# Row sums of causal attention: folding the second key tile into the first on GpSimd

## The chip, the cores and the metric

The kernel runs on one core of one Trainium2 chip. A core has five engines that run beside each other and meet through semaphores: TensorE (PE) for matmuls, VectorE (DVE), ScalarE (ACT), GpSimd (POOL), and SyncE (SP), which here only issues DMAs. The metric is the device time of one execution in microseconds; lower is better.

## What is computed

One transformer layer in fp32 on an input of 4 x 512 x 1024, with a layer norm after each half:

```python
x = layernorm(x + attention(x, wq, wk, wv, wo))   # 32 heads, 8 kv heads, head size 32, rope, causal
x = layernorm(x + ffn(x))                         # ternary gate/up/down weights with scales, 3584 wide
# attention, per batch b and head h:
scores = q @ k.T / sqrt(32) + causal_mask
attn = softmax(scores)          # exp(scores - max) / sum over the keys
out = attn @ v
```

The division by the sum over the keys is what the change is about. Every softmax row needs the sum of its exponentials over up to 512 keys.

## The kernel before

**Work and units.** The attention stage runs over 16 units `u` (4 batches x 4 groups of 8 heads). A unit has two kv heads `G`, each shared by `REP` = 4 query heads. The 32 pairs (u, G) are numbered `q = u * UG + G`, 0 to 31; the text calls each of them a head. Keys are on the partitions, queries on the free axis. The 512 keys of a head are four key tiles `j` = 3, 2, 1, 0 of 128 keys, worked on in this order. Since the mask is causal, tile j holds only the queries from 128 j on: 128, 256, 384 and 512 columns for each of the four query heads.

**One head.** For each tile TensorE computes scores (`score_k`, L984), ScalarE their exponentials into `p32[j]` (`exp`, L1139), GpSimd sets the upper triangle of the diagonal block to zero (`causal`, L1443), and TensorE multiplies with v (`pv`, L998), in fp32, four query heads on four groups of 32 columns of its array. `p32` has one buffer for each j, so the exponentials of the next head wait until all readers of the old ones are done.

**The row sums.** They are taken by TensorE too: a matmul with a matrix of ones sums over the partitions (`sums`, L1013), again fp32 and four groups of 32 columns. To spare some of it, GpSimd first adds tiles into one another (`presum`, L1451): tile 3 into the fitting columns of tile 2 (512 elements a partition), then tile 2 into tile 1 (1024 elements). So `sums` runs over tiles 0 and 1 only: 4 matmuls of 512 columns and 4 of 384, each recorded twice. The very last head has no presums and sums all four tiles.

```python
tiles = 2
if u * UG + G == NU * UG - 1:
    tiles = NT
else:
    on.wait_ge(s_pre, 2 * (u * UG + G + 1))
```

**After the sums.** VectorE transposes the sums (`sum_turn`, L1291), takes reciprocals (L1296), transposes back (L1298) and multiplies with the result of pv (`att_scale`, L1301). Only then may `pv` of tile 3 of the next head write the PSUM bank again. ScalarE and VectorE split the result into two fp16 parts (L1146, L1307), and SP stores them.

**What else runs there.** Beside the heads TensorE runs the projections of later units (`proj`, L948), scores in the other orientation for the row maxima (`score_q`, L960, L963), whose maxima VectorE takes (`row_max`, L1267), and the output projection of finished batches. VectorE and GpSimd rotate q and k (L1252 to L1254, `rope_add` L1437), ScalarE and VectorE write them as fp16 rows (L1126, L1261), and SP transposes these into the stacks. VectorE also splits incoming pages (L1231). Early on, GpSimd takes a maximum over the partitions once (`bound`, L1468).

**The order.** No engine chooses at run time. A planner in the program (`Plan`) is given every piece of work with its engine, a rank, an estimated duration and the pieces that it comes after. It walks through time and at each moment gives a free engine the ready piece of lowest rank. The resulting order is each engine's program; semaphores then enforce the dependencies. The bank `TRANS`, which `sums` writes, is taken and freed in the plan as well. After attention follows the feed-forward stage, about 740 us to the end.

## Time and profile before

| what | value |
|---|---|
| median of 3 runs (lowest, highest) | 1871.53 us (1870.84, 1872.09) |
| the profiled execution: time, span | 1868.12 us, 1866.4 us |
| mean granted TensorE clock | 0.993 of full speed |
| busy: TensorE, VectorE, ScalarE, GpSimd | 97%, 64%, 38%, 29% of the span |
| ones-matmuls for the sums (L1013), first and last start | 82.5 us, 735.5 us |

The profile is of one execution. "Busy" is the time in which an engine has an instruction running; for TensorE the ends of matmuls are modelled and records overlap. A row of a grouped view gives the line, engine and operation, output and input, how often, the busy time, the mean of one, and the idle time before them with what ended it. A timeline row gives the start and the length in microseconds; where several instructions are merged the length covers them all.

### The profile page before, as it was taken

The page shows a single profiled execution, that of the slowest core. Times are in us where ns is not written, and L with a number is a line of the kernel's source. Part 1 is how long each engine was busy: PE and PEld are TensorE (multiplying, and loading weights), DVE is VectorE, ACT ScalarE, POOL GpSimd, SP SyncE. Part 2 cuts the span into 40 slices and gives each one's busy share as a digit, 9 for nine tenths or more (in the row PEclk, how much of TensorE's full clock was granted, in tenths as well). Part 3 has the DMA queues.
Part 4 walks back from the last instruction along what each step waited for, and adds up shares of the span by engine and source line. Part 5 has one row for each costly group of instructions (what it writes and reads, how often), then busy time and mean ns, then how long its engine had stood idle before and what let it go on. Part 6 is the DMA issues. An engine that isn't in the chain of part 4 may idle for free.

```text
span 1866.4 us, 27364 instructions
## 1 busy us (share of the span) xinstructions
PE 1807.0 (97%) x10528; PEld 882.0 (47%) x10528; DVE 1187.7 (64%) x2047; ACT 710.5 (38%) x1112; POOL 543.6 (29%) x845
## 2 busy tenths in 40 slices
PE   7889999999999998999999999999999999999997
PEld 4545655555555543444444444444444444444443
DVE  7877778668768764445544444745656765667645
ACT  5443444444434444436433343342232322222221
POOL 1354546456546564131000000211321211112103
PEclk9999999999999999999999999999999999999999
DMA  8543234334334398557644353649321211232301
GB/s 246 118 103 78 54 85 125 83 80 116 90 52 114 81 212 221 209 208 263 236 171 150 107 195 126 215 148 211 127 66 53 79 66 51 72 104 85 107 12 79
DMA packets 228162, 233.13 MB, mean 125 GB/s; under 512 B 183872, under 2 KB 184128, under 8 KB 228032
## 3 DMA queue, kind: packets, MB, share of 16 engines
q1 hardware_dynamic: 227168, 230.99, 42.2%
q8 instruction: 83, 1.36, 0.3%
q10 hardware_dynamic: 864, 0.39, 0.1%
q14 instruction: 47, 0.39, 0.1%
HBM read 122.55 MB, written 72.88 MB: 105 GB/s over the span
## 4 chain that ended last, share of the span: by engine, by line
PE 85%; DVE 6%; issue 3%; SPq 2%; POOL 2%; ACT 1%; DMA 1%; ACTq 0%; DVEq 0%; POOLq 0%
PE bank L1053 31%; PE bank L948 20%; PE bank L1074 13%; PE bank L1087 6%; PE bank L998 4%; PE bank L960 3%; PE bank L984 3%; PE bank L1013 2%; SPq L1587 2%; DVE down_forms L1391 1%; PE bank L963 1%; DVE gate_blocks L1385 1%; POOL p_tiles L1451 1%; DVE row_max L1267 0%; DVE up_blocks L1375 0%
## 5 line engine op out<-in xcount | busy, mean ns | idle before, releaser
L1053 PE MATMUL bank<-x_forms,weight_forms 128*128 128x512 f16 x3136 | 700.9, 379 | 12.7 <-DVE gate_blocks L1375 4.4
L1053 PEld LDWEIGHTS bank<-x_forms,weight_forms 128*128 128x128 f16 x3136 | 305.3, 98 | 387.0 <-DVE gate_blocks L1375 7.1
L1139 ACT ACTIVATE p_tiles<-bank 128x512 f32<-128x512 f32 (+1 forms) x352 | 193.0, 556 | 276.6 <-PE bank L984 273.5
L1267 DVE TENSOR_REDUCE row_max<-bank 128x1 f32<-128x384 f32 (+3 forms) x352 | 220.0, 636 | 98.2 <-PE bank L963 96.6
L1074 PE MATMUL bank<-down_forms 128*128 128x512 f16 x1152 | 259.6, 381 | 2.4 <-issue 2.4
L948 PE MATMUL bank<-wq_parts,xT_parts 128*128 128x256 f16 x1536 | 219.4, 275 | 8.9 <-DVE wq_parts L1231 8.7
L1410 DVE TENSOR_TENSOR acc<-bank,acc 128x512 f32<-128x512 f32 x188 | 127.6, 687 | 124.2 <-PE bank L1074 64.7
L1443 POOL TENSOR_SCALAR_AFFINE_SELECT p_tiles<-p_tiles 128x128 f32<-128x128 f32 (+2 forms) x352 | 139.0, 403 | 212.2 <-ACT p_tiles L1139 210.9
L1074 PEld LDWEIGHTS bank<-down_forms 128*128 128x128 f16 x1152 | 113.0, 98 | 139.7 <-issue 4.9
L948 PEld LDWEIGHTS bank<-wq_parts,xT_parts 128*128 128x128 f16 x1536 | 144.1, 98 | 56.8 <-issue 14.2
L948 PE MATMUL bank<-wo_parts,att_parts 128*128 128x512 f16 x672 | 170.1, 382 | 0.6 <-DMA att_parts<-att_spill 0.6
L1475 POOL TENSOR_TENSOR acc<-acc,down_forms 128x1024 f32<-128x1024 f32 x16 | 38.8, 2427 | 377.4 <-DVE acc L1410 377.4
L1087 PE MATMUL bank<-down_forms 128*128 128x512 f16 x560 | 133.6, 379 | 1.7 <-DVE down_forms L1391 1.7
L960 PE MATMUL bank<-k_stack,q_stack 96*128 96x512 f16 (+3 forms) x512 | 127.0, 303 | 5.1 <-DVE row_max L1267 5.1
L984 PE MATMUL bank<-q_stack,k_stack 98*128 98x384 f16 (+3 forms) x512 | 126.4, 301 | 4.6 <-ACT p_tiles L1139 3.1
L1451 POOL TENSOR_TENSOR p_tiles<-p_tiles 128x512 f32<-128x512 f32 (+1 forms) x62 | 115.8, 1868 | 49.4 <-PE bank L998 41.3
L1375 DVE TENSOR_TENSOR up_blocks<-bank,up_blocks 128x512 f32<-128x512 f32 x84 | 57.9, 690 | 112.9 <-PE bank L1053 59.6
L1214 ACT ACTIVATE down_forms<-gate_blocks 128x512 f16<-128x512 f32 x102 | 64.0, 628 | 136.4 <-DVE gate_blocks L1385 130.4
L998 PE MATMUL bank<-p_tiles,v 128*32 128x128 f32 (+3 forms) x1024 | 95.4, 453 | 11.6 <-POOL p_tiles L1443 10.4
L1375 DVE TENSOR_TENSOR gate_blocks<-bank,gate_blocks 128x512 f32<-128x512 f32 x84 | 57.8, 688 | 74.8 <-PE bank L1053 65.0
L948 PE MATMUL bank<-wkv_parts,xT_parts 128*128 128x512 f16 x384 | 98.3, 379 | 1.3 <-DVE wkv_parts L1231 1.3
L1458 POOL TENSOR_SCALAR rstd<-rstd 128x1 f32<-128x1 f32 x96 | 34.8, 363 | 220.2 <-DVE rstd L1329 213.8
(114 smaller groups left out, 1999.9 us busy)
## 6 DMA issues: line engine op xcount, KB each, us to landing
weight_forms_spill<-weight_forms SPq DMA_DIRECT2D x28, 896.0 KB, 5.7
weight_forms<-weight_forms_spill SPq DMA_DIRECT2D x28, 896.0 KB, 4.5
x_forms_spill<-x_parts SPq DMA_DIRECT2D x56, 256.0 KB, 2.4
w_page<-gateT SPq DMA_DIRECT2D x28, 512.0 KB, 5.0
w_page<-upT SPq DMA_DIRECT2D x28, 512.0 KB, 4.0
w_page<-downT SPq DMA_DIRECT2D x28, 512.0 KB, 4.3
att_spill<-att_made SPq DMA_DIRECT2D x64, 128.0 KB, 2.1
down_forms<-x_spill SPq DMA_DIRECT2D x16, 512.0 KB, 3.4
```

The lines of the kernel that those rows point to most:

```text
L948: t = nc.tensor.matmul(dst, left[:, a, k, rows], right[:, c, k, cols], start=k == 0 and m == 0, stop=last)
L960: nc.tensor.matmul(to[:, h, :], qT[0:STK, u % QS, h0 + h, i * P:n], kT[0:STK, b % 2, kv_of(u, h0 + h), 0:n], start=h == 0, stop=False, ski ...
L984: t = nc.tensor.matmul(to[:, h, :], kT[0:STKM, b % 2, (u % UNITS) * UG + G, lo:lo + P], qT[0:STKM, u % QS, G * REP + h0 + h, lo:S], start= ...
L998: t = nc.tensor.matmul(bank[PV_BANK[q]][h * HD:(h + 1) * HD, lo:S], value, p32[j][:, h, :], start=j == NT - 1, stop=j == 0, tile_position= ...
L1053: t = nc.tensor.matmul(strassen[bank_set(use)][to][:, :], w_form[:, use % 4, A_FORMS[a_form], k * P:(k + 1) * P], xF[:, :, B_FORMS[b_form] ...
L1074: t = nc.tensor.matmul(to[:, :], hid_p[place_of(r)][:, k, a, i // 2 * P:(i // 2 + 1) * P], wd_p[place_of(r)][:, c, cols], start=r == round ...
L1087: t = nc.tensor.matmul(to[:, :], hid_f[r % NF % 3][:, HID_FORMS.index(a_form), a, pair * P:(pair + 1) * P], wd_f[r % NF % 3][:, DOWN_B[b_f ...
L1139: nc.scalar.activation(p32[j][:, h0:h0 + heads, :], bank[5 + m % 2][:, 0:heads * n].rearrange("p (h c) -> p h c", c=n), ACT.Exp, scale=SCO ...
L1267: nc.vector.tensor_reduce(mx[:, u % 2, i, h0:h0 + ROW_HEADS[i]], bank[3 + m % 2][:, 0:ROW_HEADS[i] * n].rearrange("p (h c) -> p h c", c=n) ...
L1410: nc.vector.tensor_tensor(dst, got[:, :], dst, ALU.add).then_inc(s_acc, 1)
L1443: nc.gpsimd.affine_select(out=block, in_=block, compare_op=ALU.is_ge, fill=0.0, base=0, pattern=[[0, KEY_HEADS[j]], [1, P]], channel_multi ...
L1451: nc.gpsimd.tensor_tensor(to, to, p32[j + 1][:, :, :], ALU.add).then_inc(s_pre, 1)
```

## The change

For the first 29 of the 32 heads GpSimd now also adds tile 1, which already holds tiles 2 and 3, into the last 384 columns of tile 0. It does so in two instructions, for two query heads each (768 elements a partition). `sums` then runs over tile 0 only, and waits for both. Heads 29 and 30 keep two presums and two tiles, head 31 keeps none and four. The exponentials of tile 1 of the next head wait for the second half instead of the sums; those of tile 0 still wait for the sums. In the plan `sums` gets other durations and a later rank, and the new pieces are planned at 0.2 + 768/410 us each.

```diff
+EARLY = NU * UG - 3
+PRE_EARLY, PRE_LATE = [(2, 0), (1, 0), (0, 0), (0, 1)], [(2, 0), (1, 0)]
+PRE = [PRE_EARLY if q < EARLY else PRE_LATE if q < NU * UG - 1 else [] for q in range(NU * UG)]
+PRE_BASE = [sum(len(p) for p in PRE[:q]) for q in range(NU * UG + 1)]
+def summed(q):
+    return min([j for j, _ in PRE[q]], default=NT - 1) + 1
+def added(q, j):
+    return max([p for p in PRE[q] if p[0] == j - 1], default=None)
...
-        freed = [("pv", *last, j), ("sums", *last) if j < 2 else ("presum", *last, j - 1)] if q else []
+        freed = [("pv", *last, j), ("presum", *last, *added(q - 1, j)) if added(q - 1, j) else ("sums", *last)] if q else []
...
-        final = q == NU * UG - 1
-        if j in (1, 2) and not final:
-            put(PO, at + 4, .2 + REP * (S - (j + 1) * P) / 410, "presum", u, G, j,
-                after=[("pv", u, G, j)] + [("presum", u, G, 2)] * (j == 1))
+        for n, part in enumerate(PRE[q]):
+            if part[0] == j:
+                cols = REP * (S - (j + 1) * P) / (1 if j else 2)
+                put(PO, at + 4, .2 + cols / 410, "presum", u, G, *part,
+                    after=[("pv", u, G, j)] + ([("presum", u, G, *PRE[q][n - 1])] if n else []))
...
-        put(PE, at + 3.5, 3.0 if final else 1.5, "sums", u, G, takes="T", after=[("causal", *one)] + [("presum", u, G, 1)] * (not final))
+        put(PE, at + (7 if summed(q) == 1 else 3.5), (.9, 1.6, 2.2, 2.5)[summed(q) - 1], "sums", u, G, takes="T",
+            after=[("causal", *one)] + ([("presum", u, G, *PRE[q][-1])] if PRE[q] else []))
...
-                    tiles = 2
-                    if u * UG + G == NU * UG - 1:
-                        tiles = NT
-                    else:
-                        on.wait_ge(s_pre, 2 * (u * UG + G + 1))
+                    q = u * UG + G
+                    tiles = summed(q)
+                    on.wait_ge(s_pre, PRE_BASE[q + 1])
...
-                    if j < 2:
+                    if q and added(q - 1, j):
+                        on.wait_ge(s_pre, PRE_BASE[q - 1] + PRE[q - 1].index(added(q - 1, j)) + 1)
+                    else:
                         on.wait_ge(s_sums, q)
-                    else:
-                        on.wait_ge(s_pre, 2 * q - (j - 2))
...
-                    u, G, j = which
+                    u, G, j, n = which
                     q = u * UG + G
+                    heads = slice(0, REP) if j else slice(n * REP // 2, (n + 1) * REP // 2)
                     on.wait_ge(s_pv, NT * q + NT - j)
-                    on.wait_ge(s_pre, 2 * q + 2 - j)
-                    to = p32[j][:, :, P:S - j * P]
-                    nc.gpsimd.tensor_tensor(to, to, p32[j + 1][:, :, :], ALU.add).then_inc(s_pre, 1)
+                    on.wait_ge(s_pre, PRE_BASE[q] + PRE[q].index((j, n)))
+                    to = p32[j][:, heads, P:S - j * P]
+                    nc.gpsimd.tensor_tensor(to, to, p32[j + 1][:, heads, :], ALU.add).then_inc(s_pre, 1)
```

## Rows read from the trace of the kernel before

**Rows 1.** Windows, two stretches of attention: busy us (records) by engine, clock, DMA share, GB/s

```profile
200.00:300.00 100.00, 97.66 (x801) 55.01 (x798) 77.19 (x147) 43.13 (x77) 51.26 (x87) 1.00 0.33 80
...
130.00:140.00 10.00, 8.66 (x79) 4.92 (x77) 9.86 (x17) 5.58 (x10) 7.27 (x9) 1.00 0.98 250
```

**Rows 2.** Waits of TensorE's matmuls in 120:700: total us, times, longest

```profile
PE bank L960 <- DVE row_max L1267: 4.3, 5, 1.5
```

**Rows 3.** Groups by line and form, whole span

```profile
L1451 POOL TENSOR_TENSOR p_tiles<-p_tiles 128x1024 f32<-128x1024 f32 x31 | 74.0, 2386 | 12.1 <-PE bank L998 11.2
...
L1437 POOL TENSOR_TENSOR rope_cos<-rope_cos,rope_sin 128x256 f32<-128x256 f32 x80 | 68.9, 861 | 78.1 <-DVE rope_sin L1254 77.9
...
L1261 DVE TENSOR_TENSOR stack_rows<-rope_cos,stack_rows 128x256 f16<-128x256 f32 x80 | 51.8, 648 | 11.7 <-ACT stack_rows L1126 11.5
...
L1451 POOL TENSOR_TENSOR p_tiles<-p_tiles 128x512 f32<-128x512 f32 x31 | 41.9, 1350 | 37.3 <-PE bank L998 30.1 <-issue 7.2
...
L1013 PE MATMUL bank<-p_tiles,ones 128*32 128x512 f32 x256 | 34.3, 609 | 0.0
...
L1307 DVE SCALAR_TENSOR_TENSOR att_made<-over_sum,att_made 128x512 f16<-128x512 f32 x32 | 27.3, 852 | 4.9 <-ACT att_made L1146 4.5
L1013 PE MATMUL bank<-p_tiles,ones 128*32 128x384 f32 x256 | 26.5, 486 | 0.0
```

**Rows 4.** The chain of work around one head's sums: start us, us, what

```profile
402.04 0.33 PE bank L948 x3
402.36 0.99 PE bank L998 x8
403.36 1.50 PE bank L1013 x16
```

**Rows 5.** Timeline of TensorE: pv, sums and neighbours, six stretches

```profile
93.24 1.51 PE L998 MATMUL bank<-p_tiles,v 128*32 128x384 f32 x8 [3.59 <-POOL p_tiles L1443]
...
193.83 1.69 PE L1013 MATMUL bank<-p_tiles,ones 128*32 128x512 f32 x16
...
209.43 1.69 PE L1013 MATMUL bank<-p_tiles,ones 128*32 128x512 f32 x16
...
334.66 1.06 PE L998 MATMUL bank<-p_tiles,v 128*32 128x512 f32 x8
...
336.09 1.71 PE L1013 MATMUL bank<-p_tiles,ones 128*32 128x512 f32 x16
337.73 0.83 PE L948 MATMUL bank<-wq_parts,xT_parts 128*128 128x256 f16 x6
...
402.29 1.07 PE L998 MATMUL bank<-p_tiles,v 128*32 128x512 f32 x8
403.18 1.69 PE L1013 MATMUL bank<-p_tiles,ones 128*32 128x512 f32 x16
404.79 0.50 PE L948 MATMUL bank<-wq_parts,xT_parts 128*128 128x256 f16 x3
...
408.57 0.86 PE L998 MATMUL bank<-p_tiles,v 128*32 128x128 f32 x16
```

**Rows 6.** Timeline of GpSimd: the start, and two moments of later heads

```profile
91.70 0.37 POOL L1468 PARTITION_ALL_REDUCE scale_bounds<-scale_bounds  x1 [7.00 <-issue]
...
100.60 3.74 POOL L1451 TENSOR_TENSOR p_tiles<-p_tiles 128x512 f32<-128x512 f32 x2 [7.17 <-issue]
...
200.26 1.26 POOL L1451 TENSOR_TENSOR p_tiles<-p_tiles 128x512 f32<-128x512 f32 x1 [0.68 <-PE bank L998]
...
406.22 0.41 POOL L1443 TENSOR_SCALAR_AFFINE_SELECT p_tiles<-p_tiles 128x256 f32<-128x256 f32 x1 [2.59 <-ACT p_tiles L1139]
```

**Rows 7.** Timeline of VectorE: a split of attention rows, the end of a scaling

```profile
200.28 1.79 DVE L1307 SCALAR_TENSOR_TENSOR att_made<-over_sum,att_made 128x512 f16<-128x512 f32 x1
...
406.71 0.69 DVE L1301 TENSOR_TENSOR over_sum<-bank,over_sum 128x512 f32<-128x512 f32 x1
```

**Rows 8.** Line L1261: min/median/max ns, first and last start

```profile
L1261 DVE TENSOR_TENSOR stack_rows<-rope_cos,stack_rows x80: 376/425/2569, 17.5 to 661.9; 128x256 f16<-128x256 f32 x80
```

More of the change, by code:

```diff
@@ L879, in attention_over @@
             on.wait_ge(s_exp, NU * NKEY)
-            on.wait_ge(s_pre, 2 * (NU * UG - 1))
+            on.wait_ge(s_pre, PRE_BASE[-1])
             on.wait_ge(s_sums, NU * UG)
```

## The prediction

> **What bounds the kernel now.** The page comes first: TensorE is busy for 97% of the span, GpSimd for 29%. Then the windows, because a share over the whole span hides the stages. The change lies in the attention stage, from about 65 to 740 us. There TensorE is busy for 97.66 of 100 us at 200:300, VectorE for 77.19, GpSimd for 51.26; only in short stretches, as at 130:140, does TensorE fall to 8.66 of 10, with VectorE at 9.86 [rows 1]. So between 140 and 700 us a microsecond of TensorE work taken away is nearly a microsecond of time, unless another engine's chain gets in front. The waits say how near the others are: in 120:700 the largest wait of TensorE's matmuls is 4.3 us, for the row maxima of VectorE [rows 2]. Before 140 us TensorE does stand behind GpSimd and VectorE.
>
> **Removed: the ones-matmuls of the second key tile.** The sums of a head are 16 records for two key tiles of 512 and 384 columns. By form, the 384-column ones are busy 26.5 us in 32 heads [rows 3], 0.83 us a head, but four column groups run at once and the records' ends overlap. The chain of work counts the set of 16 as 1.50 us [rows 4]. By columns that is 1.50 x 384/896 = 0.64 us for the second tile. I take 0.64, since chain pieces follow one another without overlap; 0.83 is the upper bound. 29 heads x 0.64 = 18.6 us (at most 24.1).
>
> **Moved: the sums.** They now wait for both halves on GpSimd, which start when pv of tile 0 is done, so they can't stand right behind pv 0 any more. The timeline has both cases. Adjacent: pv starts at 402.29, the sums at 403.18, the next fp16 matmul at 404.79, together 2.50 us. Apart, with three matmuls of a projection between: 334.66 to 337.73, 3.07 us [rows 5]; such a three is 0.33 us in the chain [rows 4]. 3.07 - 0.33 - 2.50 = 0.24 us for going into the 32-column fp32 matmuls and out once more. 6 of the 32 sums stand apart already, all in the first 29; for 23 it is new: 23 x 0.24 = 5.5 us lost. Against that, later sums make the scaling late, and with it pv of tile 3 of the next head (all heads but the last share one PSUM bank for pv). By then pv of tile 2 is ready too and both run in one go, as the 16 records at 408.57 do [rows 5]. 11 heads do that now, 18 of the first 29 could join; if 12 do, 12 x 0.24 = 2.9 us come back (bounds 0 and 4.3).
>
> **Added: two GpSimd adds a head.** The trace has no add of 768 elements. Between 1350 ns for 512 and 2386 ns for 1024 [rows 3], which are also its bounds, it is 1868 ns. 58 x 1.87 = 108 us on GpSimd, 3.7 us a head. Their cover is GpSimd's idle time: 51 of 100 us busy becomes about 70, and behind pv 0 it now sits idle for 2.59 us until 406.22 [rows 6]. Without the cover the price would be the 108 us themselves. What they make late: the exponentials of tile 1 of the next head on ScalarE, which wait for the second half instead of the sums; the sums, behind them VectorE's chain to the end of the scaling at 407.40 (2.6 us after the sums) [rows 7], then pv 3. Queued behind a waiting add on GpSimd are the causal masks of tiles 3 and 2, rope adds (and with them the hi and lo rows and SP's transposes into the q stack) and the small steps of the layer norm. One head's loop: adds 3.7 us with 1.9 us of masks and a rope add between them, sums 1.0, scaling 2.6, pv 3 and pv 2 0.8, pv 1 0.8, the presum of tile 1 2.4, hand-offs 1.5: 14.7 us until the next adds can start. Heads follow each other in (336.09 - 193.83)/7 = 20.3 us on average, at the shortest in 209.43 - 193.83 = 15.6 us [rows 5]. So the loop fits, with over 5 us of slack in most heads and 1 us in the shortest. I price it at 1 us in all (bounds 0 and 4).
>
> **The start.** Here GpSimd is the limit. It stands for 7.00 us before the all-reduce of the scale bounds and for 7.17 us before its next add [rows 6], and TensorE waits 3.59 us for a mask behind the first of them [rows 5]. The adds of head 0 come in just there. In front of these stalls they move all that is behind by 3.7 us; in a gap they cost nothing. I take 3.7, because GpSimd's queue has no gap between 84.7 and 105.8 but the stalls; with the adds of heads 1 and 2, in the stretch where VectorE is at 9.86 of 10, it could be 8.
>
> **VectorE behind the adds.** VectorE instructions with both inputs in SBUF are stretched under GpSimd's adds. The subtraction for the stack rows has a median of 425 ns, a minimum of 376 and a maximum of 2569 [rows 8]; one of the attention rows that starts at 200.28 lasts 1.79 us [rows 7], where a GpSimd add had started at 200.26 [rows 6]. The two forms, 80 x (0.648 - 0.376) and 32 x (0.852 - 0.679), lose 27 us under 74.0 + 41.9 + 68.9 = 185 us of GpSimd adds [rows 3]. 108 us more of them would be 16 us more of VectorE, 0.5 us a head, on an engine busy for 77 of 100. I let TensorE stand for 2 of these 16 us; the bounds are 0 and 16. The Trainium skill, page "SBUF — State Buffer", section "Who interferes with whom", says that a VectorE instruction with two SBUF inputs and a GpSimd instruction that reads SBUF block one another for the whole instruction. By that rule, the trace agrees, and it would give the third rival's time if every new add met such an instruction, against 2 us in the sum here.
>
> **The sum.** -18.6 + 5.5 - 2.9 + 1 + 3.7 + 2 = -9.3 us. The last three heads are as before, so the end of the stage moves as a whole, and the feed-forward stage keeps its work. The profiled execution took 1868.12 us (span 1866.4) and becomes 1858.8. The median of the runs shown lies 3.4 us above it at 1871.53; with the same distance the prediction is 1862.2 us.
>
> **Rivals.** *First, the hand-offs cost nothing:* the late sums find their place, the start hides head 0's adds. -18.6 + 5.5 - 4.3 = -17.4 us, with the upper price of the matmuls -23: 1849 to 1854 us. For it: TensorE nearly always has other matmuls to run. Against it: the start. *Second, it comes out even:* start 8, loop 4, VectorE 4 us: -16.0 + 16 = 0, 1871.5 us. For it: heads with 1 us of slack, and VectorE near full at 130:140 [rows 1]. Against it: 5 us of slack in most heads. *Third, slower, VectorE held by the adds:* each of the 58 adds meets a subtraction or split of VectorE and holds it for half an add, 58 x 0.93 = 54 us of VectorE. The row maxima queued behind come late, free their two score banks late, and TensorE stands for half of it, 27 us. -16.0 + 3.7 + 27 = +15 us, 1886 us. It decides once TensorE stands for more than 12 of the 54 us. For it: the stretched instructions [rows 7, 8], and that TensorE's largest wait is for the row maxima. Against it: that wait is only 4.3 us under all the adds that there are now [rows 2].
>
> **How the numbers follow.** This kernel's measurement tells about 0.2%, 3.7 us, from no change. The forecast, 4 to 15 us faster, gets 0.52; the first rival 0.14, the second 0.18, the third 0.16. So faster 0.66, same 0.18, slower 0.16. The likeliest case alone spans 1856 to 1867 us. The range for 8 in 10 takes in part of the first rival, the second, and what of the third lies just beyond it: 1851 to 1876 us.
>
> **What would show it.** Right: ones-matmuls of 384 columns in the last three heads only, 2.5 us instead of 26.5; sets of 8 records of about 0.86 us in the chain; 58 adds of 768 elements at 1.8 to 2.0 us; the sums 4 to 7 us behind pv 0; TensorE still at 97 to 100 of 100 us from 140 to 660. Wrong: a wait for the row maxima above 12 us in 120:700 (third rival); the heads after 110 us more than 4 us later than now (the start); pv 3 waiting for the scaling in many heads (the loop). A planner fixes the order on every engine from estimated durations, so the new pieces may also swap larger ones, which no step here prices.

## The result, and the profile after

The changed kernel takes 1879.24 us (median of 7 runs, 1877.5 to 1882.26) against 1871.53 us before (7 runs, 1865.5 to 1872.44): a ratio of 1.0049, 95% interval 1.0035 to 1.0064. It is 0.5% slower. The prediction was 1862.2 us, range 1851 to 1876: wrong in sign and outside the range.

First the windows of the kernel after, beside [rows 1]:

```profile
200.00:300.00 100.00, 93.59 (x748) 51.98 (x745) 77.34 (x142) 42.30 (x78) 70.84 (x96) 1.00 0.34 75
130.00:140.00 10.00, 10.00 (x76) 5.70 (x68) 9.19 (x16) 4.68 (x9) 7.30 (x11) 0.86 0.55 191
```

GpSimd went from 51.26 to 70.84 busy of 100 us, as worked out. VectorE did not move (77.19, 77.34). TensorE fell from 97.66 to 93.59: the matmul work that was taken away has turned into idle time. Then the groups by form beside [rows 3], and the statistics of one line beside [rows 8]:

```profile
L1470 POOL TENSOR_TENSOR p_tiles<-p_tiles 128x768 f32<-128x768 f32 x58 | 108.8, 1876 | 15.4 <-PE bank L1018 13.0
...
L1279 DVE TENSOR_TENSOR stack_rows<-rope_cos,stack_rows 128x256 f16<-128x256 f32 x80 | 63.4, 793 | 12.2 <-ACT stack_rows L1144 11.9
...
L1325 DVE SCALAR_TENSOR_TENSOR att_made<-over_sum,att_made 128x512 f16<-128x512 f32 x32 | 29.3, 916 | 2.1 <-ACT att_made L1164 1.9
L1031 PE MATMUL bank<-p_tiles,ones 128*32 128x384 f32 x24 | 2.5, 486 | 0.0
```

```profile
L1279 DVE TENSOR_TENSOR stack_rows<-rope_cos,stack_rows x80: 402/450/2407, 17.2 to 667.9; 128x256 f16<-128x256 f32 x80
```

The new add takes 1876 ns (1868 forecast), the 384-column ones-matmuls are down to 2.5 us, and the two VectorE forms grew by 11.6 and 2.0 us, together 13.6 where 16 were forecast. So the pieces are sized about as forecast. The waits of TensorE in 120:700, beside [rows 2]:

```profile
PE bank L980 <- DVE row_max L1285: 15.1, 16, 2.5
PE bank L991 <- DVE max_parts L1295: 4.2, 2, 3.9
PE bank L1018 <- DVE over_sum L1319: 2.3, 3, 1.1
PE bank L1004 <- ACT p_tiles L1157: 2.0, 6, 0.6
```

The wait for row maxima is above the 12 us that the prediction gave as the third rival's sign. The experiments show that it is for the most part not that rival's doing.

TensorE's timeline shows the moved sums. After, head 1 in the start and head 15 in the middle (for each pv of tile 0, the sums, and pv of tile 3 of the next head, merged with later tiles):

```profile
108.07 1.41 PE L1018 MATMUL bank<-p_tiles,v 128*32 128x512 f32 x8
...
116.70 1.07 PE L1031 MATMUL bank<-p_tiles,ones 128*32 128x512 f32 x8
...
121.05 1.50 PE L1018 MATMUL bank<-p_tiles,v 128*32 128x128 f32 x24 [0.64 <-DVE over_sum L1319]
...
408.99 1.06 PE L1018 MATMUL bank<-p_tiles,v 128*32 128x512 f32 x8
...
415.38 1.06 PE L1031 MATMUL bank<-p_tiles,ones 128*32 128x512 f32 x8
...
419.53 0.86 PE L1018 MATMUL bank<-p_tiles,v 128*32 128x128 f32 x16
```

In head 15 the sums start 6.4 us behind pv 0 (0.9 us in [rows 5]) and pv 3 of the next head 10.5 us behind it (6.3 us there). In head 1 it is 8.6 and 13.0 us. In the kernel before, the same stretch is:

```profile
105.82 1.93 PE L998 MATMUL bank<-p_tiles,v 128*32 128x512 f32 x8 [3.25 <-POOL p_tiles L1443]
...
108.44 2.09 PE L1013 MATMUL bank<-p_tiles,ones 128*32 128x512 f32 x16
...
115.19 0.43 PE L998 MATMUL bank<-p_tiles,v 128*32 128x128 f32 x8
```

That is 2.6 and 9.4 us. Over the 29 changed heads the median distance from pv 0 to the sums went from 0.9 to 6.8 us, and that to pv 3 of the next head from 6.3 to 11.3 us.

**Where the time went.** The starts of pv of tile 0, read from these timelines, give the progress of any version (us; e1 and so on are the experiments below):

```
                       head 0    head 9    head 28   head 30   0 to 9   9 to 28   28 to 30
before                  81.59    267.10    677.97    721.20    185.5    410.9     43.2
after                   81.39    277.85    685.67    731.29    196.5    407.8     45.6
e7  no new adds         80.59    264.66    666.26    711.93    184.1    401.6     45.7
e1  tiny adds           81.42    274.09    679.05    724.07    192.7    405.0     45.0
e17 tiny, sums near     80.54    262.80    667.58    709.40    182.3    404.8     41.8
```

By these marks the change gains 3.1 us in the 19 heads from 9 to 28, and loses 11.0 us in the first nine and 2.4 us in the last two. A planned order also moves pv 0 among the other matmuls, so a single mark is good to a few us: at head 8 the changed kernel is 4.4 us behind, at head 9 it is 10.8. A mark that does not move is the number of columns done in all matmuls but the sums. By it the changed kernel loses 7.7 us up to where the kernel before stands at 270 us, gains 1.2 us from there to 660 us, and loses 4.1 us from there to 750 us. Both counts agree that the loss is not spread over the stage; it sits in the start and the end, where TensorE stands still most. The windows show this together with the granted clock, first before, then after:

```profile
60.00:140.00 80.00, 68.98 (x571) 38.89 (x570) 62.69 (x121) 36.76 (x63) 41.45 (x60) 0.94 0.44 100
660.00:760.00 100.00, 92.68 (x574) 37.59 (x567) 53.65 (x101) 47.63 (x77) 48.27 (x90) 0.97 0.95 247
```

```profile
60.00:140.00 80.00, 64.51 (x518) 37.38 (x518) 64.78 (x119) 34.17 (x60) 47.98 (x63) 0.89 0.43 97
660.00:760.00 100.00, 90.67 (x559) 36.88 (x557) 56.89 (x102) 43.65 (x75) 58.65 (x94) 0.93 0.86 212
```

**Idle time and the lower clock.** The time of the attention stage can be split into three parts, worked out from one trace of each version. The stage is taken from where the kernel before stands at 60 us to where it stands at 750 us, by the columns done. "Idle" is time in which no matmul runs. "Clock" is half of the matmul time in the stretches whose granted clock was 0.5, the lower of TensorE's two levels (1.2 of 2.4 GHz); it is what these stretches cost. "Work" is the rest (us):

```
                       stage    idle    clock    work
before                 690.0    22.3     7.6    660.1
after                  700.6    40.3    14.4    645.9
e7  no new adds        682.1    28.4    13.0    640.7
e1  tiny adds          693.6    34.3    15.9    643.4
e17 tiny, sums near    678.1    28.2     3.6    646.3
e3  tiny, two tiles    704.7    32.9     8.0    663.8
```

The change takes 14.2 us of work away, and 18.0 us of idle time and 6.8 us of lower clock come in. The lower clock is no accident of the one traced run: (1 - mean granted clock) x span, averaged over the runs of a version, is 22.5 us after, 24.8 in e1, 19.4 in e7 and 13.9 in e17, and 12.9 to 14.7 in the series of the kernel before that were timed beside the experiments. No experiment changes the clock alone, so that the added idle time brings it down is argued from their coming together in the same stretches, not shown by a run of its own.

### The profile page after: what moved, and what is told of

Its sections match the earlier page's. It is cut to its first block, busy times and chain, and to the rows that moved or that the text cites. A ratio compares the mean times of both kernels' runs of the same rounds, so it can differ in the third digit from the quotient of the medians.

```text
span 1879.1 us, 26986 instructions
## 1 busy us (share of the span) xinstructions
PE 1801.7 (96%) x10296; PEld 872.9 (46%) x10296; DVE 1212.0 (65%) x2047; ACT 707.5 (38%) x1112; POOL 650.6 (35%) x903
## 4 chain that ended last, share of the span: by engine, by line
PE 81%; DVE 9%; issue 4%; POOL 2%; DMA 2%; ACT 1%; SPq 1%; ACTq 0%; DVEq 0%; POOLq 0%
PE bank L1071 31%; PE bank L968 18%; PE bank L1092 13%; PE bank L1105 6%; PE bank L1018 3%; PE bank L980 3%; PE bank L1004 3%; DVE row_max L1285 2%; PE bank L1031 2%; DVE down_forms L1409 1%; PE bank L983 1%; DVE gate_blocks L1403 1%; DMA x_forms_spill<-x_parts 1%; SPq L1606 1%; DVE x_parts L1352 1%
## 5 line engine op out<-in xcount | busy, mean ns | idle before, releaser
L1071 PEld LDWEIGHTS bank<-x_forms,weight_forms 128*128 128x128 f16 x3136 | 305.4, 98 | 389.2 <-issue 10.6
L1285 DVE TENSOR_REDUCE row_max<-bank 128x1 f32<-128x384 f32 (+3 forms) x352 | 215.9, 635 | 76.3 <-PE bank L983 74.6
L1470 POOL TENSOR_TENSOR p_tiles<-p_tiles 128x512 f32<-128x512 f32 (+1 forms) x120 | 229.2, 1910 | 72.5 <-PE bank L1018 61.3
L968 PE MATMUL bank<-wq_parts,xT_parts 128*128 128x256 f16 x1536 | 211.8, 275 | 8.8 <-DVE wq_parts L1249 8.7
L1461 POOL TENSOR_SCALAR_AFFINE_SELECT p_tiles<-p_tiles 128x128 f32<-128x128 f32 (+2 forms) x352 | 134.8, 396 | 110.1 <-ACT p_tiles L1157 108.7
L1501 POOL TENSOR_TENSOR up_blocks<-gate_blocks 128x512 f32<-128x512 f32 x10 | 12.7, 1270 | 263.4 <-DVE gate_blocks L1403 263.4
```

Source lines behind the costliest of these rows:

```text
L968: t = nc.tensor.matmul(dst, left[:, a, k, rows], right[:, c, k, cols], start=k == 0 and m == 0, stop=last)
L1071: t = nc.tensor.matmul(strassen[bank_set(use)][to][:, :], w_form[:, use % 4, A_FORMS[a_form], k * P:(k + 1) * P], xF[:, :, B_FORMS[b_form] ...
L1285: nc.vector.tensor_reduce(mx[:, u % 2, i, h0:h0 + ROW_HEADS[i]], bank[3 + m % 2][:, 0:ROW_HEADS[i] * n].rearrange("p (h c) -> p h c", c=n) ...
L1461: nc.gpsimd.affine_select(out=block, in_=block, compare_op=ALU.is_ge, fill=0.0, base=0, pattern=[[0, KEY_HEADS[j]], [1, P]], channel_multi ...
L1470: nc.gpsimd.tensor_tensor(to, to, p32[j + 1][:, heads, :], ALU.add).then_inc(s_pre, 1)
```

## The experiments

Each version is given with its ratio to the kernel before, timed beside it on the same chip.

### Taking the change apart: e1, e2, e3, e4

e1 has the order and the waits of the changed kernel, but each new add covers one column a head; e2 has three fills in place of each; e3 is e1 with a second set of ones-matmuls; e4 leaves heads 0 to 3 unfolded.

```diff
 # e1
-to = p32[j][:, heads, P:S - j * P]
-nc.gpsimd.tensor_tensor(to, to, p32[j + 1][:, heads, :], ALU.add).then_inc(s_pre, 1)
+width = S - (j + 1) * P if j else 1
+to = p32[j][:, heads, P:P + width]
+nc.gpsimd.tensor_tensor(to, to, p32[j + 1][:, heads, 0:width], ALU.add).then_inc(s_pre, 1)
 # e2, for j = 0 (three times, one after the other)
+t = nc.gpsimd.memset(p32[1][:, heads, :], 0.0)
 # e3, with the adds of e1
-tiles = summed(q)
+tiles = max(2, summed(q))        # second set: the last 384 columns of tile 0 once more
 # e4
-PRE = [PRE_EARLY if q < EARLY else ...
+PRE = [PRE_EARLY if 3 < q < EARLY else ...
```

> The changed kernel with its order, its waits and its shorter sums, but each of the 58 new GpSimd adds covers 1 column a query head (2 elements a partition) instead of 384; the row sums therefore leave out most of tiles 1 to 3. It takes the GpSimd time away (about 108 us) and nothing else. If the loss comes from that time, by whatever way (GpSimd late or VectorE held), the time falls well below the kernel before: 1871.5 - 16 to -10, ratio 0.991 to 0.995. If the loss comes from the planner's new order and the moved sums, it stays at the changed kernel's level, ratio 1.002 to 1.006. If half and half, about 1.000.

> The changed kernel, but each new add is replaced by three fills of the same half of tile 1, one after the other, so GpSimd is occupied at the same places but reads nothing from SBUF; the row sums leave out tiles 1 to 3. A look at the profile tells how long a set of three takes against 1.87 us. If VectorE held by the adds' reads is the cause, VectorE's subtraction for the stack rows goes back towards 648 ns or less, TensorE's wait for row maxima to about 4 us, and the time comes near that of the tiny adds (0.991 to 0.996). If GpSimd being late is the cause, the time stays near the changed kernel in proportion to the sets' length (1.002 to 1.006 at 1.87 us).

> As the tiny adds, but the sums multiply 512 and 384 columns again (the second set reads tile 0's last 384 columns once more, so the sums count those twice and leave out tiles 1 to 3). Against the tiny adds it gives the price of the 384-column matmuls in this order: by the chain's 0.64 us a head 18.6 us, by the busy records 24 us, and nothing if TensorE isn't the limit there. Against the kernel before it gives the price of the new order and the moved sums alone: by my terms +2.6 us for leaving and entering (5.5 - 2.9), ratio 1.001; if the order is what costs, ratio 1.006 to 1.012.

> The whole change, but heads 0 to 3 keep two presums and two tiles of sums, so 25 heads are folded. If the start is where the time is lost (heads 1 to 3 come 2 to 8 us late in the changed kernel), 6 to 9 us come back and the ratio to the kernel before is 0.999 to 1.001. If the loss is spread over the steady part, at most 2 us come back: 1.003 to 1.005.

Measured: e1 1.0030 (1.0018 to 1.0041), e2 1.0023 (1.0009 to 1.0037), e3 1.0105 (1.0086 to 1.0123), e4 1.0026 (1.0014 to 1.0039). The groups of GpSimd's new work and of VectorE's subtraction, first in e1, then in e2:

```profile
L1471 POOL TENSOR_TENSOR p_tiles<-p_tiles 128x2 f32<-128x2 f32 x58 | 12.1, 209 | 14.9 <-PE bank L1018 12.6
...
L1279 DVE TENSOR_TENSOR stack_rows<-rope_cos,stack_rows 128x256 f16<-128x256 f32 x80 | 51.0, 638 | 12.2 <-ACT stack_rows L1144 11.8
```

```profile
L1476 POOL MEMSET p_tiles<- 128x768 f32 x174 | 128.3, 737 | 20.7 <-PE bank L1019 12.3
```

Taking away 97 of the 109 us of adds changes 1.0049 into 1.0030, about 3.6 us (by the intervals 0 to 7). Putting 128 us of fills there, which only write, adds nothing to that. So GpSimd's time costs nothing measurable in this order. What is left to the adds is that they read: e2 to the changed kernel is 0.26%, with an interval that ends just above nothing. VectorE's subtractions (793 ns with adds, 638 ns with tiny ones) make 12 us of VectorE time, of which TensorE then pays at most these few us. That would be the third rival's mechanism, at about an eighth of its 27 us. With tiny adds TensorE still waits 11.1 us for the row maxima in 120:700, so most of that wait comes from somewhere else.

The large part is in e3 to before: same matmul columns as before, next to no new GpSimd work, and 1.05% (19.6 us) lost. Order and waits alone must hold it. e3 to e1, the second tile's matmuls, is 0.75%, 14 us. e4 takes back 0.23%, about 4 us, between what its two theories gave: some of the loss belongs to the first four heads, not all.

### Is it the start? e5, e6

The start of the changed kernel has one new shape: both 7 us stalls of GpSimd [rows 6] now follow each other without masks between, and TensorE waits in one piece for 8.83 us where it waited 3.59 and 3.25 us. GpSimd, then TensorE, in the kernel after:

```profile
95.84 0.37 POOL L1487 PARTITION_ALL_REDUCE scale_bounds<-scale_bounds  x1 [5.82 <-issue]
103.26 1.25 POOL L1470 TENSOR_TENSOR p_tiles<-p_tiles 128x512 f32<-128x512 f32 x1 [7.05 <-issue]
```

```profile
104.81 1.50 PE L1018 MATMUL bank<-p_tiles,v 128*32 128x384 f32 x8 [8.83 <-POOL p_tiles L1461]
```

```diff
 # e5 in the changed kernel, e6 in the kernel before: the all-reduce at the very beginning
-plan.put(VE, SLOT, .4, "bound", 0, after=[("proj", "q", 1, NT - 1, KD - 1)])
-plan.put(PO, SLOT, 3.0, "bound", 0, 0, after=[("bound", 0)])
+plan.put(VE, -300.0, .4, "bound", 0)
+plan.put(PO, -300.0, 3.0, "bound", 0, 0, after=[("bound", 0)])
```

> The whole change, but the piece that makes GpSimd stand twice for 7 us (the all-reduce of the scale bounds) is planned at the very beginning, where GpSimd has nothing to do; its results are used where they were. If the changed order's start (both stalls in one go before the masks, TensorE standing 8.8 us and then at a lower clock) is the cause of some 7 us, the ratio to the kernel before falls from 1.005 to 0.994 to 0.998, since the 3.6 + 3.3 us that the kernel before stands there go too. If the start isn't the cause it stays at 1.003 to 1.005.

> The kernel before with the same move of the all-reduce to the beginning and no other change. It takes 6.8 us of TensorE's standing and the half clock after it away: ratio 0.993 to 0.996. The distance to the changed kernel with the same move is the price of the change without its start: if the start was all of the loss, the changed one is the faster by some 5 us; if the steady part loses as well, they are equal or the changed one is slower.

Measured: e5 1.0043 (1.0026 to 1.0060), e6 0.9984 (0.9969 to 0.9999). The distance between them, 0.59%, is no smaller than that between the two kernels. The stall is not the cause, and this theory fell. e17 below has one of 8.41 us as well and is faster than before. The early all-reduce gives so little in either kernel because it makes something else late: pv 0 of head 0 starts at 92.34 us in e6 and 81.59 us before, and TensorE's first wait for VectorE's weight parts grows from 8.7 to 15.6 us.

### Removing the matmuls and nothing else: e7, and the rank alone: e8

```diff
 # e7, in the kernel before: no new adds, order untouched
-tiles = 2
+tiles = 1
 # e8, in the changed kernel: the sums get their old rank
-put(PE, at + (7 if summed(q) == 1 else 3.5), ...
+put(PE, at + 3.5, ...
```

> The kernel before with its order untouched on every engine, no new GpSimd adds, and sums over tile 0 only for all heads but the last (31 heads), right behind pv 0; the row sums leave out tiles 1 to 3. It is the gain of the removed matmuls alone. By the chain's 0.64 us a head: 20 us less, ratio 0.989; by e3 against e1 (14 us in 29 heads) 15 us, ratio 0.992; if VectorE or another engine takes over at once, 0.995 or more.

> The whole change, but the sums keep their old rank (3.5 behind the last key instead of 7), so the planner gives them TensorE as soon as the adds are done. If the late sums and with them the scaling and pv 3 are the cause of the steady loss, 3 to 6 us come back: ratio 1.001 to 1.003. If the rank does nothing, 1.004 to 1.006.

Measured: e7 0.9953 (0.9938 to 0.9968), e8 1.0064 (1.0041 to 1.0088). In the chain of work of e7, pv 0 and the sums are:

```profile
396.87 0.99 PE bank L998 x8
397.86 0.86 PE bank L1013 x8
```

1.50 us became 0.86 us: the 0.64 us of the prediction, exactly. Yet 31 heads x 0.64 = 19.8 us less matmul work made only 8.8 us. By the table of starts, heads 9 to 28 gain 9.3 us, 0.49 each; the first nine gain 1.4; and from head 28 to 30 the kernel is 2.5 us slower. The split of the stage says where the rest went: the work did get 19.4 us shorter, but TensorE stands idle for 6.1 us more, and the lower clock costs 5.4 us more (0.91 and 0.93 in 60:140 and 660:760, against 0.94 and 0.97 before). In e8 the old rank did not bring the sums back: they still start 6.8 us behind pv 0 (median), behind the adds that they wait for. The rank alone is not the cause.

### Is it an estimate of the planner? e9, e10

The planner takes a row maximum of 512 columns for 0.633 us; the trace has 0.684.

```diff
-put(VE, at + n * SLOT / NROW, .1 + ROW_HEADS[i] * (i + 1) * P / 960, "row_max", ...
+put(VE, at + n * SLOT / NROW, .15 + ROW_HEADS[i] * (i + 1) * P / 960, "row_max", ...
```

> The kernel before with one number of its planner changed: the estimate of a row-maximum instruction, 0.633 us for 512 columns, becomes 0.683 us, what the trace of the kernel before shows for it. No instruction is added or taken away; the order on the engines is planned again. Theory A (an order planned again is worth half a per cent by itself, whatever the change was): the time moves by more than 4 us, to either side, ratio outside 0.998 to 1.002. Theory B (the order matters only through what the change forces: apart sums, later GpSimd work): ratio 0.998 to 1.002, 1865 to 1873 us.

> The changed kernel with the same one number of the planner corrected (row maximum 0.683 us instead of 0.633 us). TensorE waits 15.1 us for row maxima in 120:700 in the changed kernel, 4.3 us in the kernel before. Theory A (the new order places row maxima too late, by a wrong estimate): the wait falls below 8 us and the kernel gains 5 to 9 us against the changed kernel, ratio to before 1.000 to 1.002. Theory B (the row maxima are late because VectorE is held or the moved sums put matmuls elsewhere): wait stays above 12 us, ratio 1.003 to 1.007.

Measured: e9 0.9985 (0.9973 to 0.9998), e10 1.0113 (1.0095 to 1.0131). The mended estimate leaves the wait for row maxima at 16.1 us in e10, and the kernel is 12 us slower than the changed one. e9 stays where its theory B had it; of e10's two theories neither held, since the wait stayed but the time went well beyond. What the pair does show is that the same small change of an estimate costs 12 us in the changed kernel and nothing in the kernel before. In e10 the sums of head 1 start 21.3 us behind its pv 0 (8.6 us in the changed kernel).

### Where and which way to fold: e11, e12, e13

```diff
 # e11: only heads 9 to 27
-PRE = [PRE_EARLY if q < EARLY else ...
+PRE = [PRE_EARLY if 8 < q < EARLY - 1 else ...
 # e12: tile 0's last 384 columns into tile 1, behind its exponentials; e13: e12 in heads 9 to 27 only
-on.wait_ge(s_pv, NT * q + NT - j)
+on.wait_ge(s_exp, key_n(u, G, 0, 2 * n + 1) + 1)
...
-to = p32[j][:, heads, P:S - j * P]
-nc.gpsimd.tensor_tensor(to, to, p32[j + 1][:, heads, :], ALU.add).then_inc(s_pre, 1)
+to, of = p32[1][:, heads, :], p32[0][:, heads, P:S]
+nc.gpsimd.tensor_tensor(to, to, of, ALU.add).then_inc(s_pre, 1)
```

> The changed kernel, but only heads 9 to 27 are folded by the new GpSimd adds; heads 0 to 8 and 28 keep the ones-matmuls of both key tiles. By the starts of pv of tile 0 the changed kernel is ahead of the kernel before by 3.1 us from head 9 to head 28 and behind by 10.8 us from head 0 to head 9, and by another 3 to 5 us after head 28. Theory A (the loss sits in the first heads, the middle gains): ratio 0.998 to 1.000, 1865 to 1869 us. Theory B (the loss is one of a newly planned order and shows wherever it happens to): no better than the version that leaves out four heads, ratio 1.002 to 1.005.

> The same 29 heads with the fold turned round: GpSimd adds the last 384 columns of the first key tile into the second key tile, in two halves of the heads, each as soon as the exponentials of the half are written, so that it does not wait for pv of the first tile. The ones-matmuls are 128 columns of the first tile and 384 columns of the second, 512 in all as in the changed kernel, and their set can stand right behind pv 0 again. GpSimd's work is the same. Theory A (the late, apart sums and what they push are the cost, about 15 of the 19.6 us that the order cost): 10 to 14 us better than the changed kernel, ratio 0.997 to 1.000. Theory B (any new order or the GpSimd time costs it): ratio 1.003 to 1.007 again. Theory C (GpSimd's adds now stand before the first tile's masks are needed, so they sit on the path to pv 0 and the sums): slower than the changed kernel, ratio over 1.007.

> The turned fold (GpSimd adds the last 384 columns of the first key tile into the second, right after its exponentials; sums behind pv 0) in heads 9 to 27 only; the other heads as in the kernel before. The changed fold in those heads alone gave 1.0002, the turned one in 29 heads 0.9997. Theory A (the first heads and the last ones are where a fold loses, the late sums what it loses elsewhere; the two repairs add): 0.996 to 0.998, 1863 to 1867 us. Theory B (what is left is the GpSimd time and VectorE's longer instructions, the same in any heads): 0.999 to 1.001.

Measured: e11 1.0002 (0.9990 to 1.0014), e12 0.9997 (0.9984 to 1.0010), e13 1.0007 (0.9997 to 1.0017). Each repair takes back the whole loss, and together they give no more. With the fold in the middle heads alone the expected 3 us of gain don't show in the time. In e11's trace they are there and are lost again: by the columns done it is 3.6 us ahead of the kernel before at 660 us and level with it at 750 us, with the clock at its lower level for 13.6 us between (6.8 us before). With the turned fold, where the add no longer waits for pv 0, the fold is free and worth nothing.

### The order of before, kept by force: e14, e15, e16

Here the planner first plans the kernel before, and then every piece of it must follow the piece ahead of it on its engine (except on SP). e14 frees what the change moves; e15 has the sums first, then the adds; e16 is the turned fold.

```diff
+old = planned()                  # with the pieces of the kernel before
+plan = planned(old)              # with the new ones
...
+for e, names in kept.order.items():
+    stay = [(k, *w) for k, w in names if k not in FREE and (k, w[-1]) != ("pv", NT - 1)]
+    for one, two in zip(stay, stay[1:] if e != SY else []):
+        rest = plan.pieces[two]
+        plan.pieces[two] = (e, kept.start[two], rest[2], [*rest[3], one], *rest[4:])
+FREE = ("sums", "sum_turn", "att_scale", "att_hi", "att_lo", "att_store", "presum")   # e14
```

> The changed kernel's work, every wait as in it, but the order of the kernel before is kept on TensorE, ScalarE, VectorE and GpSimd for all pieces except those that the change moves: the sums, what follows from them (turn, scaling, hi and lo rows, store), pv of tile 3 of the next head, and the new adds. Theory A (the 20 us are the accident of a newly planned order): the kept order brings it back, ratio 0.997 to 1.001. Theory B (the late sums and the waits that hang on them force it: in a kept order pv 3 and the exponentials of tile 1 of the next head come later than TensorE reaches them): slower than the changed kernel, ratio over 1.007, by the 4 to 5 us by which the sums are late in up to 29 heads perhaps up to 1.03, with TensorE waiting for the exponentials and the scaling.

> The order of the kernel before on the four engines, the sums over the first key tile alone, right behind pv of tile 0 and before the new adds, which follow the sums (so the sums leave the second key tile out, as when they were taken from the kernel before at 0.9953). GpSimd has the 58 adds of 768 elements, and the exponentials of tile 1 of the next head wait for them. Theory A (GpSimd's time and its hold on VectorE cost what was measured in the new order, 0.2 to 0.3 per cent): ratio 0.997 to 0.999. Theory B (the exponentials of tile 1, late by 4 us behind the adds, are the chain that costs): ratio 1.002 or more, with TensorE waiting for ScalarE's exponentials.

> The turned fold in 29 heads, in the order of the kernel before on TensorE, ScalarE, VectorE and GpSimd; the sums stand right behind pv 0 or as before, and wait for the second half's add, which starts when the last exponentials of the first key tile are written, beside its causal mask and pv 0. Theory A (the order planned anew costs, not the fold): better than the turned fold as planned (0.9997), 0.995 to 0.998. Theory B (the add is 1.9 us, the way from the last exponentials to the sums is 2 to 3 us with the mask in the same queue, so TensorE stands at the sums 1 to 2 us in 29 heads): ratio 1.01 to 1.03.

Measured: e14 1.0546 (1.0525 to 1.0567), e15 1.0172 (1.0152 to 1.0193), e16 1.0245 (1.0224 to 1.0267). "The new order is an accident" is refuted: the new order is what hides the change. The waits of TensorE in 120:700 of e14, and one head of it on TensorE, GpSimd and VectorE (lines there: pv L1041, sums L1054, adds L1493, scaling L1342):

```profile
PE bank L1041 <- DVE over_sum L1342: 44.2, 18, 3.5
PE bank L1003 <- DVE row_max L1308: 8.7, 12, 1.5
```

```profile
476.31 1.06 PE L1041 MATMUL bank<-p_tiles,v 128*32 128x512 f32 x8
...
482.09 1.06 PE L1054 MATMUL bank<-p_tiles,ones 128*32 128x512 f32 x8
485.84 1.05 PE L1041 MATMUL bank<-p_tiles,v 128*32 128x128 f32 x16 [2.69 <-DVE over_sum L1342]
```

```profile
477.50 3.69 POOL L1493 TENSOR_TENSOR p_tiles<-p_tiles 128x768 f32<-128x768 f32 x2 [0.70 <-PE bank L1041]
```

```profile
483.22 0.72 DVE L1332 STREAM_TRANSPOSE over_sum<-bank 128x512 f32<-128x512 f32 x1 [0.98 <-PE bank L1054]
...
485.01 0.69 DVE L1342 TENSOR_TENSOR over_sum<-bank,over_sum 128x512 f32<-128x512 f32 x1
```

Read it as a chain: pv 0 at 476.31, the adds 477.50 to 481.19, the sums at 482.09, VectorE's four steps to 485.70, and at 485.84 pv 3, for which TensorE had stood 2.69 us. The row says which dependency: the one PSUM bank of pv, free only after the scaling. 3.7 us of adds are put into a chain that TensorE reaches 6 us behind pv 0. How little room it had can be read from the trace of the kernel before: pv 3 starts 0.15 to 1.4 us after the scaling ends, 0.6 us in the median head. The 44.2 us of this wait are not all of the 102 us; by the split of the stage TensorE idles 80.5 us more than before, and the lower clock costs 32.3 us more (0.95 in 140:660, against 1.00). e15 takes the sums out of the chain, and keeps the adds ahead of the next head's masks and its exponentials of tile 1; there TensorE's largest wait is for these masks, 13.2 us in 120:700. That alone turns the 0.9953 of e7 into 1.0172; the late sums and pv 3 make it 1.0546. In e16 the adds stand ahead of the masks too, and the wait for masks is 26.6 us.

### Near and far sums: e17, e18

```diff
 # e17, in e1: the planner takes the adds of j = 0 for 0.2 us, and the sums get their old rank
-cols = REP * (S - (j + 1) * P) / (1 if j else 2)
+cols = REP * (S - (j + 1) * P) if j else 0
 # e18, in e7: the planner knows of the shorter sums
-put(PE, at + 3.5, 3.0 if final else 1.5, "sums", ...
+put(PE, at + 3.5, 3.0 if final else .9, "sums", ...
```

> As the version with the new adds cut down to one column a head (1.003), but the planner also takes these adds for short (0.2 us) and gives the sums their old rank, so that in the planned order of TensorE the sums stand 3 to 8 pieces behind pv of the first key tile instead of 12 to 26. TensorE's work is the same. Theory A (the place of the sums far behind pv 0 costs what the new order costs): 0.995 to 0.998. Theory B (any newly planned order loses it): 1.001 to 1.004.

> The kernel before without the ones-matmuls of the second key tile in 31 heads and without any new add, as at 0.9953, but the planner is told of the shorter sums (0.9 us instead of 1.5) and makes a new order, in which the sums stay 1 to 3 pieces behind pv 0. Theory A (a new order costs nothing when the sums stay near): 0.994 to 0.997. Theory B (any newly planned order loses): 0.999 to 1.003.

Measured: e17 0.9949 (0.9933 to 0.9965), e18 0.9941 (0.9923 to 0.9959). e17 and e1 give TensorE and GpSimd the same instructions; only the order differs, with the sums near or far behind pv 0. It is worth 0.8%, 15 us. Two newly planned orders with near sums are as good as the old one, so it isn't that an order is new. In e17 (pv 0, sums, pv 3):

```profile
394.91 1.06 PE L1018 MATMUL bank<-p_tiles,v 128*32 128x512 f32 x8
397.54 1.06 PE L1031 MATMUL bank<-p_tiles,ones 128*32 128x512 f32 x8
401.44 0.86 PE L1018 MATMUL bank<-p_tiles,v 128*32 128x128 f32 x16
```

pv 3 is back at 6.5 us behind pv 0. And the place of the 15 us is the start: e1 and e17 need the same 405 us from head 9 to 28, but e17 needs 182.3 us for the first nine heads and e1 192.7, and 41.8 against 45.0 us at the end. The windows, e1 first, then e17, show TensorE's idle time and the lower granted clock (0.89 against 0.94, 0.91 against 0.98) that goes with it:

```profile
60.00:140.00 80.00, 65.23 (x531) 38.09 (x534) 61.18 (x119) 34.29 (x61) 37.05 (x63) 0.89 0.40 97
...
660.00:760.00 100.00, 90.38 (x533) 35.26 (x532) 50.99 (x95) 46.11 (x76) 47.18 (x93) 0.91 0.91 233
```

```profile
60.00:140.00 80.00, 67.19 (x572) 38.91 (x572) 62.03 (x124) 36.40 (x64) 43.20 (x70) 0.94 0.43 104
...
660.00:760.00 100.00, 93.47 (x548) 38.17 (x546) 54.17 (x96) 47.94 (x77) 44.13 (x84) 0.98 0.90 246
```

By the split of the stage, e1 takes 15.5 us longer than e17, with 6.1 us more idle time, 12.3 us more cost of the lower clock and 2.9 us less work. So most of what the far sums cost arrives as the lower clock. The waits name one cause of the idle time: in 60:280 TensorE waits 8.6 us for row maxima in e1 and 1.9 us in e17.

## Why the prediction was wrong, by its steps

The measured ratios split the result into three steps, in us of 1870: the removed matmuls with near sums (e17) -9.5; the sums and what follows moved far behind pv 0 (e17 to e1) +15.1; the adds at full size (e1 to after) +3.6. Together +9.2, as measured. The sizes hold for this order of steps. By way of e3 they are +19.6 for the move with both tiles still summed, -14.0 for the matmuls and +3.6 for the adds; the move is the largest either way. And the adds cost 0.2% here, but in the turned fold, where they stand ahead of near sums, it ends at 0.9997 and not at 0.9949.

**Removed, -18.6 forecast, -9.5 measured.** The price of one head, 0.64 us, was right to the digit (e7). As matmul work it did go (19.4 us for the 31 heads of e7, 19.8 by the price). As time it is not: 0.49 us a head arrives in heads 9 to 28, next to nothing in the first nine, and 2.5 us are given back in the last heads. Over the stage, idle time and the lower clock take back 11.5 us in e7. The prediction named the stretch before 140 us as limited by others and yet counted it in full, and it had no term for the clock.

**Moved and the loop, +5.5 - 2.9 + 1 = +3.6 forecast, +15.1 measured. This is the step that failed.** The terms for going into the fp32 matmuls and out again (+5.5 - 2.9 = +2.6) are not what failed: e3 has the matmul columns of the kernel before, and its work is 3.7 us longer. What failed is the loop's price of 1 us, bounds 0 and 4. The prediction compared the length of the loop, 14.7 us, with 20.3 us between heads, and called the difference slack. But the engines work in a fixed order. What counts is when TensorE reaches the instruction that waits, and it reached pv 3 some 6 us behind pv 0 with 0.6 us to spare in the median head, against 3.7 us of adds put in: e14 shows that without a new order TensorE waits for the scaling 18 times in 120:700, and 102 us are lost in all. The planner bought that back by moving the whole cycle of a head later.

From head 9 on this is free (e1 and e17 both 405 us; e11 and e13, far and near sums in heads 9 to 27 alone, 1.0002 and 1.0007). In the first nine heads it costs 10 us and from head 28 to 30 another 3 us, where TensorE stands idle longer and runs at the lower clock longer (head 2 to 3: 15.35 us before, 19.40 after, 11.57 in e17). Every version with far sums before head 9 is slower than the kernel before (e1 to e5, e8, e10, e14), and of the freely planned ones with near sums there none is, beyond its interval (e6, e9, e11, e12, e13, e17, e18). Which instruction of a first head each microsecond goes to was not tried.

The sign that the prediction gave for the loop, pv 3 waiting for the scaling in many heads, does not show in the changed kernel (2.3 us, 3 times), because the new order hides it; the sign for the start, heads after 110 us over 4 us late, does (head 3 by 7.7 us).

**The start, +3.7 forecast.** The number is near by luck. By the table of starts the first nine heads take 3.8 us longer with the adds at full size than with tiny ones (196.5 and 192.7 us), but not by the adds of head 0 in front of the stalls, as forecast: pv 0 of head 1 is only 0.3 us later (108.07 and 107.77), and the rest comes bit by bit up to head 7. And e1 has already lost 7.2 us there to the kernel before, which the prediction had not. The joined stalls cost nothing that shows (e5, e17).

**VectorE behind the adds, +2 forecast.** About right: 2.8 us from head 9 to 28 between e1 and the changed kernel, in single traces. With the start this would be 6.6 us; the ratios give 3.6 us for both, and their intervals 0 to 7. e2 against the changed kernel (0.26%) speaks for the reads of SBUF and against GpSimd's time. The Trainium skill, page "SBUF — State Buffer", section "Who interferes with whom", names the reads of both as the condition for blocking; the trace agrees, with 793 ns under adds, 638 ns with tiny ones. Its price stayed far below the third rival's 27 us. The prediction's sign for that rival, a wait of over 12 us for row maxima, was badly chosen: it appeared (15.1 us), but the wait is 11.1 us with tiny adds, and 2.4 us with near sums as well (e17). A wait names the last link, not the cause.

**The clock, no term forecast.** The lower level of TensorE's clock costs 6.8 us more in the changed kernel's attention stage than before, and 12.3 us more in e1's than in e17's. In the traces, the changed kernel's stage is 10.6 us longer: 18.0 us of idle time and 6.8 us of lower clock, less 14.2 us of work. The prediction's sum has no row for the 6.8.

**The closing remark,** that the new pieces may swap larger ones in the planned order, "which no step here prices", was where the answer lay, but as a warning it had no number. No version with the fold that sums all keys beat the kernel before; the best, e12, is even with it. The only versions ahead of it that sum all keys are the kernel before with its all-reduce early (e6) or the mended estimate (e9), 0.15%, each with an interval that ends just below 1.

## What to carry to other kernels

Before moving work to an idle engine, ask which dependency chain it enters, not whether the engine and the cycle have room: with in-order engines the question is how long behind its producer the waiting instruction stands now. If that distance is used up, the added time must be bought by reordering, and the reordering is paid in the stretches that are short of other work, such as the start and the end of a stage. Multiply a saving only by the iterations in which that engine is the limit. And after taking work from TensorE, look at the granted clock beside the busy time: here 19.4 us of matmul work taken away, with the order untouched, brought 8.8 us, and 5.4 us of the difference was the lower clock.

## What the runs showed of the hardware

A `memset` of 768 fp32 elements a partition took 737 ns on GpSimd, the add of the same size 1876 ns. Under 128 us of such fills VectorE's subtraction for the stack rows kept a mean of 618 ns (e2), under 109 us of adds it took 793 ns, with tiny adds 638 ns. GpSimd stood for 5.82 us ahead of the partition all-reduce and for 7.05 us ahead of its next add in the changed kernel, and for 7.00 and 7.17 us in [rows 6]. With the same program, the span of the kernel before was 1860.4 us in a run with a mean granted clock of 0.996 and 1870.3 us in one with 0.989. Between 99 and 108 us of the changed kernel the granted clock was 0.50; TensorE had waited for a mask from 95.98 to 104.81 us.
